# Moving the rare stages of a software-pipelined kernel behind layer 0, and five smaller reorderings beside it

## The chip, the cores and the metric

The kernel runs on one core of a Trainium2 chip. Its engines work side by side, each through its own queue in order, and meet at semaphores: PE (TensorE, matmuls), ACT (ScalarE), DVE (VectorE), POOL (GpSimd), and SP, which here only issues DMAs. The metric is the device time of one execution in microseconds. Before the change it is 1403.78 us, the median of 3 runs (1403.2 to 1403.82).

## The reference

The input `x` is 64 x 64 x 1024 (batches, channels, length), the style vector `cond_512` 64 x 128. A block is computed in two halves.

```python
# half 1: x1 = x + S4(conv1(x));  half 2: out = x1 + FFN(conv2(x1))
for i, typ in enumerate(('same', 'upsample', 'same', 'downsample')):
    s = style @ mw.T + mb                      # modulation
    weight = SCALE * w * s[:, None, :, None]
    demod = rsqrt(sum(weight * weight, (2, 3)) + EPS)
    x = conv(x, weight * demod) + b            # kernel 3, blur of 4 taps
K = ifft(cauchy-kernel of Lambda, p, q, B, C)  # length 1024
y = irfft(rfft(u) * rfft(K)) + D * u           # S4: a causal convolution
```

The four conv layers are linear, with a style per batch. The FFN is a base matrix of 1024 x 1024 with its bias, plus a router that picks 2 of 8 experts of rank 16.

## The kernel before, in words

**Tiles and passes.** A tile is two batches (128 rows of batch and channel), so there are 32 tiles in a pass. The first pass (turns 0 to 31) does conv1 and S4 and keeps x1 in DRAM (`x1d`), the second (32 to 63) conv2 and the FFN. Float32 products are split: a value is held as a high and a low part (`a_h`, `a_l`), and each product is three matmuls, written by `product` (L1625 to L1627).

**The convolution of a tile.** Layer 0 is one product on the input (`xs_h`, `xs_l`) into the bank `ps_x`. Its output, scaled, gives `a_h`, `a_l` and, for sums of neighbouring columns, `a_f`. Layers 1 to 3 are composed on the weights into one filter per batch: `step1` and `step2` on PE with `composed1` (ACT `c_h`, DVE `c_l`) between them, eight `blurs` taps on DVE, a DMA that lays `vv` out as `vm_f`, and `composed2` (ACT `vm_h`, DVE `vm_l`). The filter is applied by `pair` (two batches) and `third`, which needs sums of filters, made by POOL (`pair_sums`, `vm_f`) and split (`vs_h` by ACT, `vs_l` by POOL). POOL's `combined` joins the three results in `vbuf`, ACT's `row_ends` sets the two outer columns, PE's `turn` transposes the tile into `ps_x` (L1742), and ACT and DVE take it from there as `u_h` and `u_l`.

**S4.** K is multiplied as a Toeplitz matrix: `s4` writes a tail, then `ps_p`, then the two halves of `ps_q`. DVE adds each to the residual `xr` as it comes (`residual`: semaphores `x1_tail`, `x1_both`, `x1_ready`).

**Turns.** Every engine runs a `body(i)`, in which work of tiles i-1 to i+2 is interleaved. The order within a body is written by hand, and it is the only thing that orders the work: an engine that waits holds all that is queued behind it. On PE a turn is pair, step2, pair, third, layer 0 of tile i+1, s4 of tile i-1, step1 of tile i+2, transposes of tile i. The transposes and layer 0 share `ps_x`, so they wait for `a_lo` and `as_sum` of tile i+1, and for `v3_fix` (row ends of tile i).

**Rare work.** Some stages run only in a few turns. `edges(i, s)` names the edge group whose stage s falls in turn i: three groups (begun in turns 1, 25 and 36) compute the outermost columns of 32 batches in four small matmuls (`edge_pe0` to `edge_pe3`), each followed by a DVE stage (`edge_ve0` to `edge_ve3`) a little later in the same turn. Group 1 has its PE stages in turns 4 to 7, group 2 in 28 to 31, group 3 in 39 to 42. `style(i, s)` does the same for the styles of the second pass: styles in turn 8, demodulation in 9, `inverse` in 11, `newton` in 12, `scales` and `shifts` in 13, `through` in 14 to 16. POOL's parts are `edge_lay` (stage 2 of an edge group), `squares(1)`, `mats_low(1)` and `tap_sums(1)`. The PE results of all these go to `ps_p`, so `edges_read` holds PE before it writes there again.

**The start.** `first_turns` sets up K (states, resolvents, transfer function, two small transforms, then through DRAM: `kout` to `kpad` to `toep`) among tile 0 and 1. `flipped` multiplies `toep` with a flipped identity, and ACT's and DVE's `toeplitz` split the result.

## Time and profile before

| | |
|---|---|
| median of 3 runs | 1403.78 us |
| the profiled execution | 1403.37 us |
| its span, first to last instruction | 1401.6 us |
| mean granted clock of PE | 0.988 |
| busy: PE, DVE, ACT, POOL | 1350.8, 948.4, 821.7, 794.3 us |
| chain that ended last: PE, DVE, ACT, POOL, issue | 85%, 7%, 4%, 2%, 1% |

The span is what the trace shows; 1.8 us of the execution lie around it. A line of the profile is named by its number in the kernel before, and operands without their buffer numbers. PE's busy time can overlap in pipelined matmuls, so gaps and the distance between equal instructions of two turns say more than the sum. The granted clock is 1.00 for 2.4 GHz and 0.50 for 1.2 GHz.

### The profile page before, as it was taken

What the parts mean: (1) busy time and instruction counts of PE and PEld (TensorE: products, weight loads), DVE (VectorE), ACT (ScalarE), POOL (GpSimd) and SP (SyncE); (2) the same over time, 40 slices, a digit from 0 to 9 for tenths busy, and PEclk for the clock granted to TensorE, in tenths of its full rate; (3) what the DMA queues carried; (4) which work ended last, traced back from release to release, by engine and by line L of the source; (5) the groups of instructions that cost most, each with busy time, mean ns of one, the idle gap of its engine ahead of it and who ended that gap; (6) DMA issues with size and microseconds to landing.
All of it is one profiled execution on the core that took longest, in us unless ns stands there. A gap on an engine that the chain in (4) does not pass through costs nothing.

```text
span 1401.6 us, 23403 instructions
## 1 busy us (share of the span) xinstructions
PE 1350.8 (96%) x8559; PEld 1276.0 (91%) x8559; DVE 948.4 (68%) x2133; ACT 821.7 (59%) x1649; POOL 794.3 (57%) x598
## 2 busy tenths in 40 slices
PE   4689899989999999999999999999999999999998
PEld 3579889989999998899999999999999999999998
DVE  7867887897777779876565766555556555555653
ACT  4467677867888787785454544545445454544530
POOL 6368666656666676565455454554545555454542
PEclk9789999999999999999999999999999999999999
DMA  4234344545445564452443423425243342524322
GB/s 135 74 102 119 93 136 129 147 116 139 134 127 134 152 148 134 119 146 88 118 106 93 128 74 111 110 78 143 74 127 94 106 115 74 145 76 123 99 80 84
DMA packets 85989, 158.64 MB, mean 113 GB/s; under 512 B 26474, under 2 KB 47859, under 8 KB 85747
## 3 DMA queue, kind: packets, MB, share of 16 engines
q1 hardware_dynamic: 84610, 155.18, 39.9%
q10 hardware_dynamic: 1264, 1.96, 0.4%
q8 instruction: 69, 1.13, 0.4%
q14 instruction: 46, 0.37, 0.1%
HBM read 94.18 MB, written 33.56 MB: 91 GB/s over the span
## 4 chain that ended last, share of the span: by engine, by line
PE 85%; DVE 7%; ACT 4%; POOL 2%; issue 1%; DMA 0%; ACTq 0%; DVEq 0%; POOLq 0%
PE psum L1625 27%; PE psum L1627 26%; PE psum L1626 26%; PE psum L1742 4%; DVE vv L1411 1%; DVE a_l L1423 1%; ACT xin L1001 1%; PE psum L271 1%; DVE a_f L1428 1%; ACT u_h L1057 0%; ACT xs_h L1006 0%; DVE de L355 0%; ACT vbuf L1045 0%; POOL xs_l L858 0%; PE psum L1906 0%
## 5 line engine op out<-in xcount | busy, mean ns | idle before, releaser
L833 POOL TENSOR_TENSOR vbuf<-vbuf 128x512 f32<-128x512 f32 x64 | 97.5, 1523 | 303.3 <-ACT vbuf L1052 303.1
L1625 PE MATMUL psum<-wt_h,u_h 128*128 128x386 f32 (+1 forms) x760 | 261.0, 343 | 0.0
L1627 PE MATMUL psum<-wt_h,u_l 128*128 128x386 f32 (+1 forms) x760 | 258.2, 340 | 0.0
L1626 PE MATMUL psum<-wt_l,u_h 128*128 128x386 f32 (+1 forms) x760 | 257.6, 339 | 0.0
L1423 DVE SCALAR_TENSOR_TENSOR a_l<-psum,tabs,a_h 128x512 fp32r<-128x512 f32 x128 | 95.1, 749 | 126.3 <-ACT a_h L1020 125.8
L847 POOL TENSOR_TENSOR vm_f<-vm_f 128x512 f32<-128x512 f32 x64 | 82.8, 1294 | 167.4 <-DVE vm_l L1417 167.4
L1625 PE MATMUL psum<-a_h,vm_h 128*128 128x256 f32 x512 | 154.8, 302 | 4.2 <-ACT vbuf L1045 4.2
L1045 ACT ACTIVATE vbuf<-psum,tabs 128x512 f32<-128x512 f32 x128 | 105.0, 820 | 85.3 <-PE psum L1627 85.2
L1057 ACT ACTIVATE u_h<-psum 128x1024 fp32r<-128x1024 f32 x64 | 65.5, 1024 | 147.5 <-PE psum L1742 147.4
L858 POOL TENSOR_TENSOR xs_l<-xin,xs_h 128x1024 fp32r<-128x1024 f32 x64 | 141.4, 2210 | 12.9 <-ACT xs_h L1006 12.9
L1411 DVE SCALAR_TENSOR_TENSOR vv<-psum,vv 128x192 f32<-128x192 f32 (+2 forms) x384 | 137.2, 357 | 13.2
L1626 PE MATMUL psum<-a_l,vm_h 128*128 128x256 f32 x512 | 146.0, 285 | 0.0
L1627 PE MATMUL psum<-a_h,vm_l 128*128 128x256 f32 x512 | 145.5, 284 | 0.0
L1626 PEld LDWEIGHTS psum<-wt_l,u_h 128*128 128x128 f32 x760 | 143.6, 189 | 1.2
L1625 PEld LDWEIGHTS psum<-wt_h,u_h 128*128 128x128 f32 x760 | 143.6, 189 | 1.3
L1627 PEld LDWEIGHTS psum<-wt_h,u_l 128*128 128x128 f32 x760 | 143.2, 188 | 0.0
L1506 DVE TENSOR_TENSOR xo<-psum,xo 128x250 f32<-128x250 f32 (+2 forms) x90 | 40.6, 506 | 124.6 <-PE psum L1627 124.6
L878 POOL TENSOR_TENSOR xo<-xr,xo 128x1024 f32<-128x1024 f32 x32 | 85.3, 2666 | 63.1 <-DMA xo<-in_b_base_dram 63.1
L1437 DVE TENSOR_TENSOR u_l<-psum,u_h 128x1024 fp32r<-128x1024 f32 x64 | 78.4, 1224 | 54.5 <-ACT xo L1061 38.4
L1625 PEld LDWEIGHTS psum<-a_h,vm_h 128*128 128x128 f32 x512 | 98.1, 192 | 12.5 <-ACT vbuf L1045 11.9
L1625 PE MATMUL psum<-xs_h,m_h 128*128 128x512 f32 x256 | 104.3, 407 | 0.0
L837 POOL TENSOR_TENSOR vbuf<-vbuf 128x512 f32<-128x512 f32 x64 | 98.9, 1546 | 5.0
(306 smaller groups left out, 4056.8 us busy)
## 6 DMA issues: line engine op xcount, KB each, us to landing
vm_f<-vv SPq DMA_DIRECT2D x256, 112.0 KB, 2.6
xin<-in_x_ph_dram SPq DMA_DIRECT2D x32, 512.0 KB, 4.5
xr<-in_x_row_dram SPq DMA_DIRECT2D x32, 512.0 KB, 5.0
x1d<-xr SPq DMA_DIRECT2D x64, 256.0 KB, 3.3
xin<-x1d SPq DMA_DIRECT2D x32, 512.0 KB, 5.1
xr<-x1d SPq DMA_DIRECT2D x64, 256.0 KB, 5.7
xo<-in_b_base_dram SPq DMA_DIRECT2D x32, 512.0 KB, 3.9
out_dram<-xo SPq DMA_DIRECT2D x31, 512.0 KB, 3.0
```

The costliest lines, as they stand in the source:

```text
L833: G.tensor_tensor(v3[:, :, 1:H:2], v3[:, :, 1:H:2], by_odd, ALU.subtract).then_inc(v3_odd, 1)
L837: G.tensor_tensor(v3[:, :, 0:H:2], v3[:, :, 0:H:2], by_odd, ALU.add).then_inc(v3_val, 1)
L847: G.tensor_tensor(vs_f, vm_f[:, :, :, 0, :], vm_f[:, :, :, 1, :], ALU.add).then_inc(vs_sum, 1)
L858: G.tensor_tensor(xs_l[:, :, 1:H + 1], xin[:, :, :], xs_h[:, :, 1:H + 1].bitcast(F32), ALU.subtract).then_inc(in_lo, 1)
L878: G.tensor_tensor(xo[:, :].rearrange("p (n q) -> p n q", q=2), xr[:, :, :].rearrange("p q n -> p n q"), xo[:, :].rearrange("p (n q) -> p n ...
L1045: A(view(vbuf, H * b, (2 * H + b - H * b, 2), (2, Q)), ps_pair.rearrange("p (r m) -> p r m", r=2), ACT.Identity, scale=tab(c, t, b, T_S4), ...
L1411: V.scalar_tensor_tensor(out=to, in0=src[:, k0:k1 + 1:2, :], scalar=BOTH[j], in1=to, op0=ALU.mult, op1=ALU.add).then_inc(blur, 1)
L1423: V.scalar_tensor_tensor(out=by_parity(a_l, b), in0=ps_x[:, b, :].rearrange("p (m r) -> p r m", r=2), scalar=tabs[:, c, T_S1, batch(t, b)] ...
L1437: V.tensor_tensor(u_l[:, :, :, :].rearrange("m k b c -> m b k c"), ps_x[:, :, :].rearrange("m b (k c) -> m b k c", c=C), u_h[:, :, :, :].r ...
L1625: nc.tensor.matmul(to, stat_h, mov_h, start=first_ and n == 0, stop=False, skip_group_check=True)
L1626: nc.tensor.matmul(to, stat_h, mov_l, start=False, stop=False, skip_group_check=True)
L1627: ins = nc.tensor.matmul(to, stat_l, mov_h, start=False, stop=end, skip_group_check=True)
```

## The change

1. **Inserted stages.** On DVE the rare stages are gathered in `inserted(i)`. In the second pass it stands where they stood, ahead of `layer0(i + 1)`; otherwise behind it, ahead of `composed2(i + 1)`. Their PE results go to `ps_late`, the second half of `ps_q`, so PE's test that they are read (`edges_read`) moves from ahead of `s4` to ahead of its last third, and in the second pass to ahead of `ffn(2)`. Their PE stages wait for `x1_ready` in place of `x1_both`.
2. **Residual.** `residual` is cut in two, and `composed1(i + 2)` stands between them.
3. **POOL.** `edge_lay`, `squares(1)`, `mats_low(1)` and `tap_sums(1)` stand behind `combined` and ahead of `pair_sums(i + 1)`; the last two also come in other turns (4 and 8, before 2 and 4).
4. **K's flip** stands ahead of the transposes of tile 0, and ACT's `row_ends(0)` ahead of `column_sums(1)`.
5. **The start.** `pair(0, 1)` comes whole ahead of `transform`, the two thirds go between K's small transforms, layer 0 of tile 1 ahead of `edge_pe3`; DVE's `through(0, 2)` and `variances(0)` come earlier, POOL's `tap_sums(0)` goes ahead of `mats_low(0)`, ACT's `m0_h` ahead of `rate_times_roots`, and SP loads `cm` ahead of `w3`.

```diff
@@ -597,8 +597,10 @@
-    ps_style, ps_demod = (ps_step, ps_p), (ps_p, ps_p)
-    ps_beta = (ps_q[:, 0, :], ps_p)
+
+    ps_late = ps_q[:, 1, :]
+    ps_style, ps_demod = (ps_step, ps_late), (ps_p, ps_late)
+    ps_beta = (ps_q[:, 0, :], ps_late)
...
@@ -646,8 +648,8 @@
                 sp.dma_start(mwT[:, 0, :, :].rearrange("p a b -> p (a b)"), d["mod_w"][:, 0:NL * P]).then_inc(style_in, 16)
+                sp.dma_start(cmf[:, 0, :, :].rearrange("p b c -> p (b c)"), d["cm"][:, 0:NCM * P]).then_inc(cm_in, 16)
                 sp.dma_start(w3T[:, :, :, :].rearrange("p a b c -> p (a b c)"), d["w3"]).then_inc(w3_in, 16)
-                sp.dma_start(cmf[:, 0, :, :].rearrange("p b c -> p (b c)"), d["cm"][:, 0:NCM * P]).then_inc(cm_in, 16)
...
@@ -806,8 +808,8 @@
             squares(0)
+            tap_sums(0)
             mats_low(0)
-            tap_sums(0)
...
@@ -867,8 +869,6 @@
                     pair_sums_low(i)
                 if first(i - 1):
                     sum_low(i - 1)
-                for e in edges(i, 2):
-                    edge_lay(nc, pool, sh, e)
                 if here(i):
                     combined(i)
                 if second(i - 1):
...
@@ -877,6 +877,15 @@
                                     xo[:, :].rearrange("p (n q) -> p n q", q=2), ALU.add).then_inc(xo_ready, 1)
+
+                for e in edges(i, 2):
+                    edge_lay(nc, pool, sh, e)
+                if turn_is(i, 1):
+                    squares(1)
+                if turn_is(i, 4):
+                    mats_low(1)
+                if turn_is(i, 8):
+                    tap_sums(1)
                 if turn_is(i, -1):
                     folded(1, fold1())
                     folded(2, fold3())
...
@@ -890,12 +899,6 @@
                     if here(i + 2):
                         inputs(i + 2)
-                if turn_is(i, 1):
-                    squares(1)
-                if turn_is(i, 2):
-                    mats_low(1)
-                if turn_is(i, 4):
-                    tap_sums(1)
...
@@ -954,9 +957,9 @@
             mats_high(0)
             roots_of(0)
-            rate_times_roots()
             act.wait_ge(m0_in, 16)
             A(m0_h[:, :, :, :], m0f[:, :, :, :], ACT.Copy).then_inc(mats_hi, 1)
+            rate_times_roots()
             act.wait_ge(fold_in, 32)
...
@@ -1086,11 +1089,11 @@
                 third_evacuated(0)
                 layer0(1)
                 composed2(1)
+                row_ends(0)
                 column_sums(1)
                 pads(1)
                 inputs(2)
                 inputs_high(2)
-                row_ends(0)
                 composed1(2)
...
@@ -1452,6 +1457,8 @@
                 ve.wait_ge(s4_both, at(g))
                 V.tensor_tensor(xr[:, :, :], ps_p.unsqueeze(1).to_broadcast([P, 2, H]), xr[:, :, :], ALU.add)\
                     .then_inc(x1_both, 1)
+
+            def residual_last(g):
                 ve.wait_ge(x1_both, at(g))
                 ve.wait_ge(s4_done, at(g))
                 V.tensor_tensor(xr[:, :, :], ps_q[:, :, :], xr[:, :, :], ALU.add).then_inc(x1_ready, 1)
...
@@ -1516,6 +1523,7 @@
                 step_rate()
                 variances(0)
+                step_scaled()
                 inverse(0)
                 newton(0)
...
@@ -1533,12 +1541,12 @@
                 edge_ve0(nc, ve, sh, 0, ps_p)
                 through(0, 1)
                 resolvents()
+                through(0, 2)
                 state_halves()
                 composed1(1)
                 resolvents_scaled()
                 layer0(0)
                 composed2(0)
-                through(0, 2)
                 transfer()
                 edge_ve1(nc, ve, sh, 0, ps_p)
...
@@ -1552,6 +1560,29 @@
+
+            def inserted(i):
+                for e in edges(i, 1):
+                    if e > 1:
+                        ve.wait_ge(sh.edge_in, 64 * (e - 1))
+                    edge_scale(nc, ve, sh, e, sh.xg[:, :, :] if e > 1 else xgA[:, EB:B, :])
+                for k, stage in enumerate((edge_ve0, edge_ve1, edge_ve2, edge_ve3)):
+                    for e in edges(i, 3 + k):
+                        stage(nc, ve, sh, e, ps_late)
+                if style(i, -3):
+                    styles(1)
+                if style(i, -2):
+                    variances(1)
+                if style(i, 0):
+                    inverse(1)
+                if style(i, 1):
+                    newton(1)
+                if style(i, 2):
+                    scales(1)
+                    shifts(1)
+                for l in range(3):
+                    if style(i, 3 + l):
+                        through(1, l)
...
@@ -1576,37 +1607,23 @@
...
-                    if style(i, 3 + l):
-                        through(1, l)
+                if second(i - 1):
+                    inserted(i)
                 if here(i + 1):
                     layer0(i + 1)
+                if not second(i - 1):
+
+                    inserted(i)
                 if second(i - 1):
                     router(place(i - 1)[1])
                 if here(i + 1):
                     composed2(i + 1)
                 if first(i - 1):
-                    residual(i - 1)
+                    residual_first(i - 1)
                 if here(i + 2):
                     composed1(i + 2)
+                if first(i - 1):
+                    residual_last(i - 1)
...
@@ -1758,6 +1766,8 @@
                 if g == 0:
                     pe.wait_ge(toep_lo, 3)
                 for to, done, tb, stat in ((ps_p, s4_both, 0, None), (ps_q[:, 0, :], None, 1, 0), (ps_q[:, 1, :], s4_done, 2, 1)):
+                    if stat == 1:
+                        edges_read(i)
                     for j in range(3):
                         st = (s_h[:, j, :], s_l[:, j, :]) if stat is None else rows(2 * j + stat)
...
@@ -1799,8 +1809,6 @@
                     pe.wait_ge(ssq_ready, 2)
                 if style(i, -2):
                     pe.wait_ge(var_ready, 2)
-                if turn_is(i, 1):
-                    pe.wait_ge(sh.edge_step, sh.edge_read[0, 3])
...
@@ -1820,26 +1828,24 @@
                 resolved()
                 pair(0, 0)
                 step2(1)
+                pair(0, 1)
                 transform()
-                pair_begins(0, 1)
+                third(0, 0)
                 twisted()
-                pair_ends(0, 1)
+                third(0, 1)
                 second_transform()
                 edge_pe2(nc, pe, sh, 0, ps_p)
-                third(0, 0)
-                third(0, 1)
+                layer0(1)
                 pe.wait_ge(folds, 2)
                 edge_pe3(nc, pe, sh, 0, ps_p)
-                layer0(1)
                 pe.wait_ge(blur, at(1, NBLUR, NBLUR - 1))
                 step1(2)
+                flipped()
                 pe.wait_ge(a_lo, at(1, 2, 1))
                 pe.wait_ge(as_sum, at(1))
                 turn(0)
 
             def body(i):
-                if turn_is(i, 1):
-                    flipped()
...
@@ -1854,12 +1860,12 @@
                         if i - 2 < TILES:
-                            pe.wait_ge(x1_both, i - 1)
+                            pe.wait_ge(x1_ready, i - 1)
                         else:
                             pe.wait_ge(out_ready, i - 1 - TILES)
-                        stage(nc, pe, sh, e, ps_p)
+                        stage(nc, pe, sh, e, ps_late)
                 if any(style(i, k) for k in (-3, -2, 3, 4, 5)):
-                    pe.wait_ge(x1_both, i - 1)
+                    pe.wait_ge(x1_ready, i - 1)
...
@@ -1876,8 +1882,9 @@
                 if first(i - 1):
                     if i > 1:
                         pe.wait_ge(x1_ready, i - 1)
-                    edges_read(i)
-                    s4(i - 1)
+                    else:
+                        pe.wait_ge(sh.edge_step, sh.edge_read[0, 3])
+                    s4(i - 1, i)
...
@@ -1889,7 +1896,6 @@
                         pe.wait_ge(out_ready, t)
-                    edges_read(i)
                     (ffn_by_parts(i - 1) if turn_is(i - 1, LAST) else ffn(0)).then_inc(pe_gate, 1)
...
@@ -1920,6 +1926,7 @@
                     else:
+                        edges_read(i)
                         ffn(2)
                         pe.wait_ge(hwT_lo, t + 1)
```

DVE in turn 12, Newton's step. L1186 to L1189 and, in the changed kernel, L1189 to L1192 are `newton(1)`; `a_l`, `a_f` are layer 0 of tile 13, `vm_l` its filter. Before:

```order
L1574 TENSOR_TENSOR wt_l<-wst,wt_h 128x320 [waits w_hi]
L1186 TENSOR_TENSOR dema<-dem 128x256
L1187 TENSOR_TENSOR dema<-dema,demt 128x256 [waits chain]
L1188 TENSOR_SCALAR dema<-dema 128x256 [waits chain]
L1189 SCALAR_TENSOR_TENSOR dem<-dem,dema 128x256 [waits chain]
L1423 SCALAR_TENSOR_TENSOR a_l<-psum,tabs,a_h 128x2x256 [waits a_hi,chain]
L1423 SCALAR_TENSOR_TENSOR a_l<-psum,tabs,a_h 128x2x256 [waits a_hi]
L1428 SCALAR_TENSOR_TENSOR a_f<-psum,tabs,a_f 128x256 [waits a_odd]
L1428 SCALAR_TENSOR_TENSOR a_f<-psum,tabs,a_f 128x256
L1417 TENSOR_TENSOR vm_l<-vm_f,vm_h 128x512 [waits vm_hi] x2
L1449 TENSOR_TENSOR xr<-psum,xr 128x2x128 [waits s4_tail,xr_in]
L1453 TENSOR_TENSOR xr<-psum,xr 128x1024 [waits s4_both,x1_tail]
```

and now:

```order
L1605 TENSOR_TENSOR wt_l<-wst,wt_h 128x320 [waits w_hi]
L1428 SCALAR_TENSOR_TENSOR a_l<-psum,tabs,a_h 128x2x256 [waits a_hi] x2
L1433 SCALAR_TENSOR_TENSOR a_f<-psum,tabs,a_f 128x256 [waits a_odd]
L1433 SCALAR_TENSOR_TENSOR a_f<-psum,tabs,a_f 128x256
L1189 TENSOR_TENSOR dema<-dem 128x256
L1190 TENSOR_TENSOR dema<-dema,demt 128x256 [waits chain]
L1191 TENSOR_SCALAR dema<-dema 128x256 [waits chain]
L1192 SCALAR_TENSOR_TENSOR dem<-dem,dema 128x256 [waits chain]
L1422 TENSOR_TENSOR vm_l<-vm_f,vm_h 128x512 [waits vm_hi,chain]
L1422 TENSOR_TENSOR vm_l<-vm_f,vm_h 128x512 [waits vm_hi]
L1454 TENSOR_TENSOR xr<-psum,xr 128x2x128 [waits s4_tail,xr_in]
L1458 TENSOR_TENSOR xr<-psum,xr 128x1024 [waits s4_both,x1_tail]
```

Newton's four instructions have passed from ahead of `a_l` to between `a_f` and `vm_l`.

POOL in turn 1. `vbuf` is `combined`, `wsq` and `wsqT` are `squares(1)`, `vm_f` is `pair_sums(2)`. Before:

```order
L835 TENSOR_TENSOR vbuf<-vbuf 128x2x255 [waits v3_odd]
L837 TENSOR_TENSOR vbuf<-vbuf 128x512 [waits v3_odd]
L847 TENSOR_TENSOR vm_f<-vm_f 128x2x256 [waits vm_lo]
L862 TENSOR_TENSOR as_l<-a_f,as_h 128x2x256 [waits as_hi]
L858 TENSOR_TENSOR xs_l<-xin,xs_h 128x2x512 [waits in_hi]
L781 TENSOR_TENSOR wsq<-wT 64x768 [waits wT1_in]
L783 TENSOR_TENSOR wsq<-wsq 64x4x64 [waits wsq_step]
L786 TENSOR_TENSOR wsqT<-wsq 64x4x64 [waits wsq_step]
L786 TENSOR_TENSOR wsqT<-wsq 64x4x64
L853 TENSOR_TENSOR vs_l<-vm_f,vs_h 128x512 [waits third_done,vs_hi]
```

and now:

```order
L837 TENSOR_TENSOR vbuf<-vbuf 128x2x255 [waits v3_odd]
L839 TENSOR_TENSOR vbuf<-vbuf 128x512 [waits v3_odd]
L783 TENSOR_TENSOR wsq<-wT 64x768 [waits wT1_in]
L785 TENSOR_TENSOR wsq<-wsq 64x4x64 [waits wsq_step]
L788 TENSOR_TENSOR wsqT<-wsq 64x4x64 [waits wsq_step]
L788 TENSOR_TENSOR wsqT<-wsq 64x4x64
L849 TENSOR_TENSOR vm_f<-vm_f 128x2x256 [waits vm_lo]
L864 TENSOR_TENSOR as_l<-a_f,as_h 128x2x256 [waits as_hi]
L860 TENSOR_TENSOR xs_l<-xin,xs_h 128x2x512 [waits in_hi]
L855 TENSOR_TENSOR vs_l<-vm_f,vs_h 128x512 [waits third_done,vs_hi]
```

The squares have passed from behind `xs_l` to ahead of `pair_sums(2)`.

PE at the end of `first_turns`. `dt,flip` is K's flip, `ident,vbuf` the transposes of tile 0, `a_h,vm_h` the first pair of tile 1. Before:

```order
L1626 MATMUL psum<-x_l,cm_h 128x192
L1627 MATMUL psum<-x_h,cm_l 128x192
L1742 MATMUL psum<-ident,vbuf 128x128 [waits v3_fix,as_sum,a_lo]
L1742 MATMUL psum<-ident,vbuf 128x128 x7
L1675 MATMUL psum<-dt,flip 128x512 [waits toep_in]
L1675 MATMUL psum<-dt,flip 128x512
L1625 MATMUL psum<-a_h,vm_h 128x256 [waits vm_lo,vm_hi,a_pad]
```

and now:

```order
L1643 MATMUL psum<-x_l,cm_h 128x192
L1644 MATMUL psum<-x_h,cm_l 128x192
L1692 MATMUL psum<-dt,flip 128x512 [waits toep_in]
L1692 MATMUL psum<-dt,flip 128x512
L1750 MATMUL psum<-ident,vbuf 128x128 [waits v3_fix,as_sum,a_lo]
L1750 MATMUL psum<-ident,vbuf 128x128 x7
L1642 MATMUL psum<-a_h,vm_h 128x256 [waits vm_lo,vm_hi,a_pad]
```

The flip, which waits for K's DMA, now stands ahead of the transposes.

## Rows read from the trace of the kernel before

**Rows 1.** Waits of PE: engine, line, waited for, total us, times, longest us.

```profile
PE psum L1625 <- POOL vs_l L853: 4.5, 2, 2.4
PE psum L1625 <- DVE c_l L1384: 4.3, 5, 1.1
```

**Rows 2.** Timeline of PE: start us, us, instruction, count, idle before and releaser; L1742.

```profile
72.07 1.94 PE L1742 MATMUL psum<-ident,vbuf 128*128 128x128 f32 x8 [5.28 <-ACT vbuf L1038]
...
93.27 1.04 PE L1742 MATMUL psum<-ident,vbuf 128*128 128x128 f32 x8
...
129.46 1.04 PE L1742 MATMUL psum<-ident,vbuf 128*128 128x128 f32 x8
...
204.02 1.04 PE L1742 MATMUL psum<-ident,vbuf 128*128 128x128 f32 x8
...
270.07 1.04 PE L1742 MATMUL psum<-ident,vbuf 128*128 128x128 f32 x8
...
323.35 1.04 PE L1742 MATMUL psum<-ident,vbuf 128*128 128x128 f32 x8
...
388.38 1.04 PE L1742 MATMUL psum<-ident,vbuf 128*128 128x128 f32 x8
...
532.04 1.04 PE L1742 MATMUL psum<-ident,vbuf 128*128 128x128 f32 x8
...
603.17 1.04 PE L1742 MATMUL psum<-ident,vbuf 128*128 128x128 f32 x8
```

**Rows 3.** Chain that ended last, second pass, L1742: start us, us, what.

```profile
766.62 0.87 PE psum L1742 x8
...
869.64 0.87 PE psum L1742 x8
...
894.23 0.87 PE psum L1742 x8
```

**Rows 4.** Timelines of DVE, POOL and PE in a steady turn of the first pass.

```profile
397.97 0.75 DVE L1423 SCALAR_TENSOR_TENSOR a_l<-psum,tabs,a_h 128x512 fp32r<-128x512 f32 x1 [1.64 <-ACT a_h L1020]
...
400.02 0.87 DVE L1428 SCALAR_TENSOR_TENSOR a_f<-psum,tabs,a_f 128x256 f32<-128x256 f32 x2
...
400.81 1.28 DVE L1417 TENSOR_TENSOR vm_l<-vm_f,vm_h 128x512 fp32r<-128x512 f32 x2
...
391.46 1.29 POOL L853 TENSOR_TENSOR vs_l<-vm_f,vs_h 128x512 fp32r<-128x512 f32 x1 [0.64 <-ACT vs_h L995]
...
402.17 1.30 POOL L847 TENSOR_TENSOR vm_f<-vm_f 128x512 f32<-128x512 f32 x1 [1.43 <-DVE vm_l L1417]
...
393.67 0.28 PE L1625 MATMUL psum<-as_h,vs_h 128*128 128x256 f32 x1
```

**Rows 5.** DVE: L1187 twice in its timeline, then busy time in four windows.

```profile
18.67 0.43 DVE L1187 TENSOR_TENSOR dema<-dema,demt 128x256 f32<-128x256 f32 x1
...
278.39 1.63 DVE L1187 TENSOR_TENSOR dema<-dema,demt 128x256 f32<-128x256 f32 x1
...
19.90:21.35 1.45, 1.30 (x8) 1.00 0.00 0
23.08:24.20 1.12, 1.02 (x7) 1.00 0.03 7
159.25:164.30 5.05, 4.83 (x8) 1.00 0.04 13
295.70:301.55 5.85, 5.64 (x15) 1.00 0.53 148
```

**Rows 6.** The start: SP's and PE's timelines, then PE, granted clock in a window.

```profile
63.97 0.34 SPq L668 DMA_DIRECT2D dt<-kpad  x1
...
73.81 3.52 PE L1675 MATMUL psum<-dt,flip 128*128 128x512 f32 x4
...
81.04 0.39 PE L1625 MATMUL psum<-a_h,vm_h 128*128 128x256 f32 x1 [0.96 <-ACT vbuf L1045]
...
70.00:72.00 2.00, 0.00 (x0) 0.57 0.00 0
```

More of the change, by code:

```diff
@@ L1284, in step_rate, with step_scaled @@
                 link(V.tensor_scalar(stpi[:, :], stpi[:, :], 23, None, ALU.logical_shift_left))
+            def step_scaled():
                 V.tensor_tensor(rate, stpi[:, :].bitcast(F32), pp, ALU.mult).then_inc(rate_ready, 1)
@@ L1444, in even_and_odd, with residual_first @@
                                 s_odd.rearrange("m j b c -> m b j c"), ALU.add).then_inc(sum_ready, 1)
-            def residual(g):
+            def residual_first(g):
                 ve.wait_ge(xr_in, 16 * (g + 1))
@@ L1578, in body @@
                                            op0=ALU.mult, op1=ALU.subtract).then_inc(bt_lo, 1)
-                for e in edges(i, 1):
-                    if e > 1:
-                        ve.wait_ge(sh.edge_in, 64 * (e - 1))
-                    edge_scale(nc, ve, sh, e, sh.xg[:, :, :] if e > 1 else xgA[:, EB:B, :])
-                for k, stage in enumerate((edge_ve0, edge_ve1, edge_ve2, edge_ve3)):
-                    for e in edges(i, 3 + k):
-                        stage(nc, ve, sh, e, ps_p)
-                if style(i, -3):
-                    styles(1)
-                if style(i, -2):
-                    variances(1)
-                if style(i, 0):
-                    inverse(1)
-                if style(i, 1):
-                    newton(1)
-                if style(i, 2):
-                    scales(1)
-                    shifts(1)
-                for l in range(3):
-                    if style(i, 3 + l):
-                        through(1, l)
+                if second(i - 1):
+                    inserted(i)
                 if here(i + 1):
                     layer0(i + 1)
+                if not second(i - 1):
+                    inserted(i)
                 if second(i - 1):
@@ L1706, in step2, with pair @@
                 ins.then_inc(step2_done, 1)
-            def pair_begins(g, b):
+            def pair(g, b):
                 if b == 0:
@@ L1715, in pair_begins @@
                 pe.wait_ge(vm_lo, at(g, 2, b))
-                columns(g, b, 0)
-            def columns(g, b, r):
-                o = (EVEN, 1)[r]
-                return product(ps_pair[:, Q * r:Q * r + Q],
-                               [(vm_h[:, b, P * (2 * k + r):P * (2 * k + r) + P], vm_l[:, b, P * (2 * k + r):P * (2 * k + r) + P],
-                                a_h[:, b, o + k:o + k + Q], a_l[:, b, o + k:o + k + Q]) for k in range(2)], True, True)
-            def pair_ends(g, b):
-                columns(g, b, 1).then_inc(pair_done, 1)
-            def pair(g, b):
-                pair_begins(g, b)
-                pair_ends(g, b)
+                for r, o in ((0, EVEN), (1, 1)):
+                    ins = product(ps_pair[:, Q * r:Q * r + Q],
+                                  [(vm_h[:, b, P * (2 * k + r):P * (2 * k + r) + P], vm_l[:, b, P * (2 * k + r):P * (2 * k + r) + P],
+                                    a_h[:, b, o + k:o + k + Q], a_l[:, b, o + k:o + k + Q]) for k in range(2)], True, True)
+                ins.then_inc(pair_done, 1)
             def third(g, b):
@@ L1746, in rows, with s4 @@
                 return (u_h[:, k, :, :].rearrange("p b c -> p (b c)"), u_l[:, k, :, :].rearrange("p b c -> p (b c)"))
-            def s4(g):
+            def s4(g, i):
                 pe.wait_ge(pair_out, at(g + 1, 2, 1))
```

## Prediction

> **What bounds the kernel now.** The waits of the tensor engine come first: PE is busy for 1350.8 of 1401.6 us (the page), and its single waits are short [rows 1]. Then the starts of its eight transposes, once a turn, say where those waits lie [rows 2]. From 388.38 to 532.04 us nine turns take 143.66 us: 15.96 us a turn, gapless, so in an undisturbed turn only matmuls count, and nothing here removes a matmul. The loss lies in five places, each worked out against 15.96 a turn.
> - The start: transposes of tile 0 at 72.07, after 5.28 us idle.
> - Turns 2 and 3 (93.27 to 129.46): 36.19, so 4.3 too long, 3.8 of it in turn 2.
> - Turns 4 to 7, the first edge group (129.46 to 204.02): 74.56, less 4 x 15.96, 10.7 too long. The same four edge stages cost PE 4.7 as pure matmul work in the second pass: from 766.62 to 869.64 is 103.02 against 4 x 24.59 [rows 3]. So 6.0 is waiting.
> - Turns 12 to 14, Newton's step, scales and shifts (270.07 to 323.35): 53.28 less 47.88 is 5.4, of which about 0.6 is the constant's own matmuls: 4.8.
> - Turns 28 to 31, the second edge group (532.04 to 603.17): 71.13 less 63.84 less 4.7 is 2.6.
> Together with the start some 22 us are to be had, no more.
>
> **The inserted stages.** In a steady turn whose transposes start at 388.38, the order on the vector engine is a_l, column sums a_f (end 400.89, 12.5 after the transposes), vm_l (end 402.09), residual; then POOL's pair_sums, as_l, xs_l and vs_l follow from vm_l. POOL starts vs_l of this chain after an idle of 0.64, and has it 0.92 before PE begins the third that reads it (391.46 + 1.29 = 392.75 against 393.67) [rows 4]. So a stage of length X put between a_f and vm_l holds PE by X - 1.56. Before, X stood ahead of a_l: there idle times of the vector engine (1.64 ahead of the first a_l [rows 4], 0.64 ahead of the second) swallow 2.3 of it, but what is left delays a_f, on which the transposes, ACT's column sums, the next inputs and c_h hang; PE then waited for c_l [rows 1].
> By that alone the new place is worse for equal X, since it has no idle time to hide in. What decides is X itself. The same instruction (L1187, 128x256) took 0.43 us when POOL was quiet and 1.63 beside POOL's combination of a tile [rows 5]. The scales and shifts took 1.45 and 1.12 at the start, and 5.85 as one piece in turn 13; the second stage of an edge took 5.05 in turn 5 [rows 5]. The new place lies where POOL has finished the combination and waits for vm_l, so I take the quiet durations: 2.6 for scales and shifts; for the edge stages, Newton and the like the same ratio (2.6/5.85 = 0.44) gives 2.2 for the 5.05, and about 2.1 each for the first edge stage and Newton. The others are under 1.8. The bounds are both ends of the ratio, 0.44 and 1.
> Waiting after: 0.6 + 0.6 + 0.1 per edge group, call it 1.5 with small change; 1.0 for scales, 0.5 for Newton, 0.2 for the reciprocal: 1.7. Gains: first edge group 6.0 - 1.5 = 4.5 (its worst wait, 2.4 for vs_l [rows 1], came from tap_sums, see below); turns 12 to 14: 4.8 - 1.7 = 3.1; second edge group 2.6 - 1.5 = 1.1. Sum 8.7.
> The Trainium skill (SBUF, State Buffer; section Who interferes with whom) gives a reason for the two durations: VectorE and GpSimd share a port pair as an exclusive lock, and a vector instruction with two SBUF inputs blocks against a GpSimd instruction that reads SBUF, for its whole length. L1187 agrees. The same rule speaks against the change at POOL's moved pieces, below.
>
> **POOL's moved pieces.** squares(1) (3.8 us behind xs_l, the cause of turn 2's wait of 2.1 for vs_l), mats_low(1), tap_sums(1) and the edge layouts now stand between the combination and pair_sums, where POOL idles 1.4 in a steady turn [rows 4]. What is longer pushes pair_sums and so vs_l, with 1.56 allowed. squares(1): 3.8 - 1.4 = 2.4 late, stall 0.8 without interference; beside vm_l (two instructions, 1.28 together [rows 4]) up to 1.3 more. I take a stall of 1.5: 0.6 gained. Turn 2's other 1.7 is clock: the idle before it was followed by a stretch at half clock as in [rows 6]; with a wait still there I count half of it back. Gain 1.4 (0.3 to 3.0). mats_low and tap_sums now fall into turns whose inserted stage delays vm_l anyway, at 0 to 0.8. The edge layouts (about 3 us) had idle time ahead of the combination and lose it: 3.0 - 1.4 - 1.56 is 0, with vm_l's 1.28 in it 1.3, at two turns. I take 1.2 for all of this, range 0 to 3.5. By the skill's rule taken at its word the upper ends hold, and this part alone would come to about +2.
>
> **The residual.** composed1's c_l now runs ahead of the last sum. Steady: c_l at 405.1 to 405.65, last sum to 406.9, and the next u_l starts at 406.9 (390.97 one turn on). It fits without a gap; 0, and if it did not, u_l has several us until layer 0. SP's x1 store starts 1.9 later, its reader is a turn off. The tests of the edge banks move from the head of the S4 product into its third part, 3.9 us later, which covers the later reads; the second pass keeps its order.
>
> **The start.** Three small things: variances no longer wait for step_scaled, POOL has tap_sums done before Newton's multiply, so the scales come 2 to 3 us earlier, but ACT, busy without a gap from 14.1 to 21.7, allows only 0.9 of it. through(0,2) leaves a crowded place and costs 0.9 in a quiet one instead of 2.5. The transfer function so starts about 2.1 earlier, and K's way with it, since blurs(1), which SP's vm copies and then K's DMAs follow, ends on the same chain. pair(0,1), 2.9 us on PE, goes into PE's wait of 3.3 us for atv. K's second DMA was issued at 63.97 [rows 6], with 3.4 to landing in the list of DMAs: 67.4, now about 65.3. PE has nothing from about 62 on, and K's flip, now ahead of tile 0's transposes, holds these till K is there. Flip 3.5 [rows 6] at half clock (the level of 1.2 GHz), 1.8 at full; transposes 1.9 [rows 2] or 1.0. ACT's row_ends(0), moved ahead of inputs(2), is no longer what they wait for. They end at 68.0 to 70.6, ACT's u_h then follows, and with toeplitz() behind it the evacuation that PE's next pair needs ends 5.0 later: 73.2 to 75.7 instead of 81.0 [rows 6]. Gain 5.3 to 7.8; I take 6.0, near the half-clock end, because the clock fell to half 4 us into the idle before [rows 6].
>
> **The sum.** 8.7 + 1.4 - 1.2 + 6.0 = 14.9; turn 3's half us comes back, 0.3: 15.2. The profiled execution took 1403.37 (span 1401.6 and 1.8 around it), 0.4 under the median 1403.78. So 1388.4.
>
> **Rivals.**
> A, the late chain: the inserted stages keep their long durations. Then behind a_f they cost 4.7 - 1.56, 5.05 - 1.56, 2.0 and so on: 8 per edge group against 6.0 and 2.6, and 3.3 + 4.3 against 4.8 in turns 12 to 14. That is 10 worse than before, and each of about six waits over 2 us may pull the clock to half for 2.7 us, 1.4 lost each, 8 in all. Against it 7.4 from start and turn 2: 1403.4 + 18 - 7.4 = 1414. It decides from an average X of about 3.5, where it would be even. For it: every one of these stages was long in the trace. Against it: POOL idle there.
> B, K holds the transposes: the DVE chain does not shorten, K lands at 67.4 as before, flip and transposes run at half clock to 72.8, gain at the start 3; POOL's pieces at their upper end, 3.5: total gain 3 + 0.3 + 8.7 - 3.5 = 8.5, so 1394.9.
> C, everything goes well: clock at full through the start (7.8), turn 2 wholly cured (3.8), edge layouts free (0): 8.7 + 7.8 + 3.8 + 1.5 = 21.8 and 1381.6.
> D, no change: the freed time is taken by another wait, c_l and x1_tail both, which have 1.0 and 2.7 of room. Stage lengths around 3.5, within 0.2%.
>
> **Chances.** Forecast 0.58, B 0.17, C 0.14, A 0.06, D 0.05. A difference under 0.2% (2.8 us) can't be told from none. Faster 0.91, same 0.04, slower 0.05. The range reaches from C to B: 1381.5 to 1396.
>
> **What would show it.** Right: transposes of tile 0 at 66 to 69 with the flip in front; turn 2 within 18.3; turns 4 to 7 together at 70; Newton's L1187 line at 0.4 us; PE's waits for vs_l short but more of them, those for c_l nearly gone. Wrong: vector copies over 0.6 us behind a_f, waits for vm_l or for x1_tail, or a steady turn above 16.0.

## The result, and the profile after

The changed kernel takes 1426.67 us (median of 4 runs, 1426.44 to 1426.93), the kernel before 1403.49 (4 runs, 1403.15 to 1403.82): a ratio of 1.0165 [1.0148, 1.0183]. The forecast was 1388.4, with a range to 1396.0. The profiled execution has a span of 1424.8 us, 23.2 more than before, at a mean granted clock of 0.994.

The chain of waits of the changed kernel, shares of the span by engine and then by line. Before, PE had 85% of it.

```profile
PE 56%; DMA 14%; ACT 10%; DVE 10%; SPq 4%; issue 4%; POOL 2%; ACTq 0%; DVEq 0%; POOLq 0%
PE psum L1642 18%; PE psum L1644 17%; PE psum L1643 17%; DMA vm_f<-vv 10%; DMA x1d<-xr 4%; SPq L723 3%; ACT xin L1004 2%; DVE vv L1416 2%; PE psum L1750 2%; ACT xs_h L1009 2%; DVE xr L1464 2%; ACT as_h L994 1%; ACT c_h L983 1%; DVE u_l L1442 1%; SPq L680 1%
```

DMAs, which had 0% before, now hold 14%: the copies of the blurred filter (`vm_f<-vv`) and the store of x1 (`x1d<-xr`). PE's waits say the same from its side, beside [rows 1] (line, waited for, total us, times, longest us):

```profile
PE psum L1642 <- DVE c_l L1389: 17.5, 21, 1.1
PE psum L1642 <- ACT vbuf L1048: 12.1, 28, 2.2
PE psum L1642 <- POOL vs_l L855: 2.6, 3, 1.6
```

Then PE's transposes in turns where nothing rare happens, which before stood 15.96 apart [rows 2]:

```profile
424.94 1.06 PE L1750 MATMUL psum<-ident,vbuf 128*128 128x128 f32 x8
443.22 0.95 PE L1750 MATMUL psum<-ident,vbuf 128*128 128x128 f32 x7 [0.38 <-ACT vbuf L1041]
461.40 0.85 PE L1750 MATMUL psum<-ident,vbuf 128*128 128x128 f32 x6 [0.27 <-ACT vbuf L1041]
```

18.28 and 18.18 us (x7 and x6: records that are missing from the trace). From turn 17 to turn 27 each turn is 1.1 to 2.3 longer than before, 1.8 on average. One such turn on SP's queue, on DVE and on ACT (rows left out are marked):

```profile
447.91 1.27 SPq L680 DMA_DIRECT2D x1d<-xr  x2
449.23 0.67 SPq L700 DMA_DIRECT2D xin<-in_x_ph_dram  x1
452.32 0.33 SPq L705 DMA_DIRECT2D xr<-in_x_row_dram  x1
452.75 2.44 SPq L723 DMA_DIRECT2D vm_f<-vv  x4
...
443.44 1.22 DVE L1458 TENSOR_TENSOR xr<-psum,xr 128x1024 f32<-128x1024 f32 x1
446.20 0.55 DVE L1389 SCALAR_TENSOR_TENSOR c_l<-psum,tabp,c_h 128x320 fp32r<-128x320 f32 x1 [1.54 <-ACT c_h L983]
446.67 1.22 DVE L1464 TENSOR_TENSOR xr<-psum,xr 128x1024 f32<-128x1024 f32 x1
...
450.11 2.32 DVE L1416 SCALAR_TENSOR_TENSOR vv<-psum,vv 128x256 f32<-128x256 f32 x6
...
464.37 0.55 DVE L1389 SCALAR_TENSOR_TENSOR c_l<-psum,tabp,c_h 128x320 fp32r<-128x320 f32 x1 [1.62 <-ACT c_h L983]
...
459.04 1.40 ACT L990 ACTIVATE vm_h<-vm_f 128x512 fp32r<-128x512 f32 x2 [3.08 <-DMA vm_f<-vv]
```

It is a closed loop. From `c_l` (446.20) DVE goes on to the last sum, `u_l` and the blurs; these end at 452.43, and SP issues the copies at 452.75, 6.55 behind `c_l`. ACT's `vm_h` waits for them and starts at 459.04, 6.29 later. From there ACT works without a wait through its inputs to `c_h`, and the next `c_l` starts at 464.37, 5.33 behind `vm_h`. 6.55 + 6.29 + 5.33 = 18.17, a turn (18.18). The x1 store hangs on the same `c_l`: the last sum stands behind it, the store is issued at 447.91, SP issues the load of `xr` when the store has landed (452.32), and the copies right behind that load. Before, the same two paths were these:

```profile
386.50 1.22 DVE L1453 TENSOR_TENSOR xr<-psum,xr 128x1024 f32<-128x1024 f32 x1
...
389.14 0.55 DVE L1384 SCALAR_TENSOR_TENSOR c_l<-psum,tabp,c_h 128x320 fp32r<-128x320 f32 x1 [0.16 <-ACT c_h L980]
...
393.28 2.31 DVE L1411 SCALAR_TENSOR_TENSOR vv<-psum,vv 128x256 f32<-128x256 f32 x6
...
389.01 1.27 SPq L678 DMA_DIRECT2D x1d<-xr  x2
390.84 0.33 SPq L698 DMA_DIRECT2D xin<-in_x_ph_dram  x1
393.08 0.33 SPq L703 DMA_DIRECT2D xr<-in_x_row_dram  x1
395.63 2.52 SPq L721 DMA_DIRECT2D vm_f<-vv  x4
```

From the sum before the last to the store it was 389.01 - 386.50 = 2.51, and it is 447.91 - 443.44 = 4.47 now: the split sends the store 1.96 later. What SP waited for between 400 and 550 us, before and then after:

```profile
SPq L703 <- DMA x1d<-xr: 17.6, 9, 2.1
SPq L721 <- DVE vv L1411: 17.4, 9, 2.1
```

```profile
SPq L705 <- DMA x1d<-xr: 17.4, 8, 2.4
```

Before, SP had the load of `xr` out and then stood 1.9 us a turn ready to issue the copies, waiting for DVE's blurs. After, that wait is gone: the load goes out just when the blurs end, and the copies right behind it. Medians of the eleven steady turns 17 to 27, in us; the last column is experiment 3 below:

| | before | changed | 3 |
|---|---|---|---|
| `c_l` to the issue of the copies | 6.48 | 6.29 | 6.49 |
| end of the blurs to that issue | 0.03 | 0.06 | 0.03 |
| issue of `xr`'s load to that issue | 2.44 | 0.45 | -2.46 (behind it) |
| issue of the copies to `vm_h` | 3.65 | 6.29 | 3.64 |
| `vm_h` to the next `c_l` | 5.87 | 5.14 | 5.88 |
| turn | 15.96 | 17.76 | 16.00 |

So the copies are not issued late: at most 0.50 behind the end of the blurs in the changed kernel, 0.14 on average. They land late, `vm_h` starts 2.6 us later behind their issue than before, when the 512 KB of `xr` go out 0.45 ahead of them. With the old 3.65 the loop would be 6.29 + 3.65 + 5.14 = 15.1 (an estimate from the table) and would hide under PE's 15.96. The profile's chain of waits goes through the x1 store in 12 turns between 230 and 630 us and through DVE's blurs in 10; the slow copies are in all of them.

### The profile page after: what moved, and what is told of

Same layout as the page of the kernel before. It is cut to its first block, busy times and chain, and to the rows that moved or that the text cites. A ratio compares the mean times of both kernels' runs of the same rounds, so it can differ in the third digit from the quotient of the medians.

```text
span 1424.8 us, 23407 instructions
## 1 busy us (share of the span) xinstructions
PE 1353.3 (95%) x8559; PEld 1274.1 (89%) x8559; DVE 916.6 (64%) x2133; ACT 817.1 (57%) x1649; POOL 795.6 (56%) x598
## 3 DMA queue, kind: packets, MB, share of 16 engines
q10 hardware_dynamic: 1264, 1.96, 0.4%
q8 instruction: 69, 1.13, 0.3%
## 4 chain that ended last, share of the span: by engine, by line
PE 56%; DMA 14%; ACT 10%; DVE 10%; SPq 4%; issue 4%; POOL 2%; ACTq 0%; DVEq 0%; POOLq 0%
PE psum L1642 18%; PE psum L1644 17%; PE psum L1643 17%; DMA vm_f<-vv 10%; DMA x1d<-xr 4%; SPq L723 3%; ACT xin L1004 2%; DVE vv L1416 2%; PE psum L1750 2%; ACT xs_h L1009 2%; DVE xr L1464 2%; ACT as_h L994 1%; ACT c_h L983 1%; DVE u_l L1442 1%; SPq L680 1%
## 5 line engine op out<-in xcount | busy, mean ns | idle before, releaser
L835 POOL TENSOR_TENSOR vbuf<-vbuf 128x512 f32<-128x512 f32 x64 | 97.5, 1524 | 297.8 <-ACT vbuf L1055 297.8
L990 ACT ACTIVATE vm_h<-vm_f 128x512 fp32r<-128x512 f32 x128 | 76.8, 630 | 80.4 <-DMA vm_f<-vv 79.6
L1422 DVE TENSOR_TENSOR vm_l<-vm_f,vm_h 128x512 fp32r<-128x512 f32 x128 | 85.0, 703 | 28.8 <-ACT vm_h L990 28.1
```

The source lines that it names most:

```text
L835: G.tensor_tensor(v3[:, :, 1:H:2], v3[:, :, 1:H:2], by_odd, ALU.subtract).then_inc(v3_odd, 1)
L990: A(vm_h[:, b, :], vm_ff[:, b, :], ACT.Copy).then_inc(vm_hi, 1)
L1422: V.tensor_tensor(vm_l[:, b, :], vm_ff[:, b, :], vm_h[:, b, :].bitcast(F32), ALU.subtract).then_inc(vm_lo, 1)
```

## The experiments

The names: S, the split closes the loop through SP's queue; P, the inserted stages behind layer 0 are the loss; D, `c_l` ahead of the last sum hurts on DVE itself. All ratios are to the kernel before, run on the same chip. This D is not rival D of the prediction.

**1. The change, the last sum whole again.**

```diff
-                if here(i + 2):
-                    composed1(i + 2)
                 if first(i - 1):
                     residual_last(i - 1)
+                if here(i + 2):
+                    composed1(i + 2)
```

> The changed kernel, but the residual's last sum stands ahead of composition's low part again; all else as changed. Theory S (the split closes a loop through SP: last sum, x1 store, its completion, xr load, vm copies, vm_h, vm_l, c_h, c_l, last sum, about 18 us long in the changed kernel's trace): the first pass goes back to 15.96 us a turn, 26 turns x about 1.1 to 1.8 come back, 1395 to 1402. Rival P (the inserted stages and POOL's pieces behind layer 0 are what lengthens the turns): it stays at 1420 or above.

1394.41 us (1393.52 to 1395.13), ratio 0.9943 [0.9926, 0.996]. Steady turns take 15.96 to 16.03. That is 0.6 under the range expected. Two lines in another order cost 32.3 us (the kernel before took 1403.27 beside this run and 1403.49 beside the change); P is refuted, and the rest of the change is worth about 9.

**2. The split alone, in the kernel before.** `residual` cut in two with `composed1` between, nothing else.

```diff
                 if first(i - 1):
-                    residual(i - 1)
+                    residual_first(i - 1)
                 if here(i + 2):
                     composed1(i + 2)
+                if first(i - 1):
+                    residual_last(i - 1)
```

> The kernel before, with nothing changed but the split of the residual: composition's low part ahead of the last sum. Theory S: undisturbed turns of the first pass rise from 15.96 to 17.5 to 18.2 us, total 1425 to 1440. Rival P: within 3 us of the kernel before.

1434.11 us (1433.41 to 1434.63), ratio 1.0227 [1.0209, 1.0245]. PE's transposes of two steady turns:

```profile
414.76 1.06 PE L1746 MATMUL psum<-ident,vbuf 128*128 128x128 f32 x8
432.52 1.04 PE L1746 MATMUL psum<-ident,vbuf 128*128 128x128 f32 x8
450.87 1.06 PE L1746 MATMUL psum<-ident,vbuf 128*128 128x128 f32 x8 [0.46 <-ACT vbuf L1038]
```

17.76 and 18.35: the loop is there without any other part of the change, with the same numbers (load to copies 0.45, copies to `vm_h` 6.30).

**3. The change with its split; on SP the load of `xr`, with its wait for the store, goes behind the copies.** The arithmetic engines' orders are those of the change.

```diff
-                if first(i - 1):
-                    _, t = place(i - 1)
-                    if t:
-                        sp.wait_ge(x1_out, 32 * t)
-                    sp.dma_start(xr[:, :, :], ...)
...
                                          vv[HALF[b], :, :]...).then_inc(vm_in[b], 16)
+                if first(i - 1):
+                    _, t = place(i - 1)
+                    if t:
+                        sp.wait_ge(x1_out, 32 * t)
+                    sp.dma_start(xr[:, :, :], ...)
```

> The changed kernel with its split, but on SP the xr load (with its wait for the end of the x1 store) is issued behind the vm copies in place of ahead of them. Theory S: the loop is open, DVE's copies' wait falls away, turns of 16.0 to 16.4 us, 1397 to 1410, though the residual then waits for xr. Rival D (the split costs on DVE itself, by the later u_l and blurs, not through SP): turns stay at 17.5 and more, 1420 or above.

1392.80 us (1392.13 to 1393.45), ratio 0.9931 [0.9914, 0.9948]. SP's queue in a steady turn, and PE:

```profile
379.70 1.28 SPq L680 DMA_DIRECT2D x1d<-xr  x2
381.02 0.68 SPq L700 DMA_DIRECT2D xin<-in_x_ph_dram  x1
384.49 2.92 SPq L718 DMA_DIRECT2D vm_f<-vv  x4
387.45 0.58 SPq L724 DMA_DIRECT2D xr<-in_x_row_dram  x1
...
425.23 1.04 PE L1750 MATMUL psum<-ident,vbuf 128*128 128x128 f32 x8
441.22 1.04 PE L1750 MATMUL psum<-ident,vbuf 128*128 128x128 f32 x8
```

The time is 4 us under the range expected. The copies wait for the blurs again and the turn is 15.99. D is refuted, since DVE's order is the same here. S holds in that the cost comes through SP's queue: the split is harmless once the load that waits for its store stands behind the copies. The median time from issue to landing of one copy went with it, from 4.4 in the changed kernel (2.6 before) to 2.3 here:

```profile
vm_f<-vv SPq DMA_DIRECT2D x36, 112.0 KB, 4.4
```

```profile
vm_f<-vv SPq DMA_DIRECT2D x40, 112.0 KB, 2.3
```

The table above separates two parts of the cure. The time of issue gave little, 0.14 us a turn on average. The landing gave 2.6. That it is the 512 KB right ahead that slow the copies rests on their nearness in time in these kernels; no run changes the size of that load, so what is shared stays open.

**4. As 1, with two edits of the start undone:** `mats_low(0)` ahead of `tap_sums(0)` on POOL, SP's `w3` ahead of `cm`.

> As the run with the last sum ahead, and besides POOL's mats_low(0) ahead of tap_sums(0) and SP's w3 ahead of cm, as in the kernel before. If DVE's ssq (2.56 us in the changed kernel, 0.42 before) was held by POOL's row of tap sums, ssq falls back to 0.4 to 0.6 and everything up to tile 0 comes about 2 us earlier: 1 to 2.5 us under the run with the last sum ahead. If the 2 us come from elsewhere, no difference.

1393.93 us (1392.37 to 1394.36), ratio 0.9938 [0.9925, 0.9952]: no difference from 1 that could be told. The transposes of tile 0 come 1.1 earlier (69.42 for 70.52), but those of tile 1 only 0.4.

**5 to 8: parts alone.** 5 is the kernel before with part 1 of the change, 6 with parts 4 and 5, 7 is experiment 1 with part 3 undone, 8 is experiment 1 with SP's copies first.

> The kernel before with part 1 of the change alone: the inserted stages behind layer 0, their PE results in ps_late, the tests of the edge banks and the waits for x1_ready with it. The prediction gave this part 8.7 us (first edge group 4.5, turns 12 to 14 3.1, second edge group 1.1), so 1394.6. Read from the trace of the change with the whole sum (first edge group 71.03 us for 74.56, turns 12 to 14 50.65 for 53.28, second group 71.13 for 71.13, turn 9 0.5 longer) it is worth 3.5 + 2.6 + 0 - 0.5 = 5.6, so 1397.7, and somewhat less here, since tap_sums(1) still stands behind xs_l in turn 4 and holds the same vs_l that an inserted stage holds: 1397.7 to 1400. The rival theory that inserted stages behind layer 0 cost (late chain) says 1404 or more.

> The kernel before with the start alone: K's flip ahead of tile 0's transposes, row_ends(0) early, and all of part 5. The prediction gave it 6.0 us: 1397.3. Read from the trace of the change with the whole sum, the first pair of tile 1 starts at 76.55 for 81.04 (4.5 earlier), but the transposes of tile 1 start at 90.26 for 93.27 (3.0 earlier), so 1.5 of it is given back in turn 0 to waits for DVE and SP that the flip had covered: 3.0, and 1400.3. The rival of the prediction in which K alone holds the transposes says 3.0 as well, with the flip waiting for K's DMA; it differs in that the first pair would start 3 earlier, not 4.5.

> The change with the whole sum, and POOL's moves undone: edge_lay ahead of combined, squares(1), mats_low(1), tap_sums(1) behind xs_l in turns 1, 2 and 4. If POOL's moves bring what the prediction gave turn 2 and cost what it gave the layouts (1.4 and 1.2), the time stays within 1 us of the 1394.4 of the change with the whole sum, with turn 2 near 20.2 instead of 18.65 us and a turn with an edge layout shorter. If the moves matter more (tap_sums(1) in turn 4 behind xs_l plus an inserted stage), it is 1396 to 1398. If the gap between the gains predicted (14.9) and found (9) lies in POOL's pieces, it is 1391 or less.

> The change with the whole sum, and SP's load of xr with its wait for the x1 store behind the vm copies. If the loop through SP's queue was the only thing that the split cost, then with copies first it no longer matters where the sum stands: 1392.8 to 1394.4, the 1392.8 of the split with copies first plus up to 1.6 for PE's few waits for c_l, which the split had cured. If the early xr load itself (its own wait for the store) cost something in the change with the whole sum too, this is clearly below 1394.4, at 1391 to 1392.5. If the xr load comes too late behind the copies, steady turns exceed 16.0 and it is above 1395.

| | us | ratio | turn of 146.55 before |
|---|---|---|---|
| 5, inserted stages alone | 1402.83 (1398.59 to 1404.47) | 1.0002 [0.9989, 1.0015] | 23.62 |
| 6, start alone | 1400.72 (1397.53 to 1402.31) | 0.9988 [0.9977, 0.9999] | 20.21 |
| 7, both, POOL as before | 1401.68 (1397.02 to 1403.66) | 0.9996 [0.9982, 1.001] | 23.56 |
| 8, all with the whole sum, copies first | 1394.38 (1392.16 to 1397.02) | 0.9948 [0.9931, 0.9964] | 17.53 |
| before | 1402.84 (1399.03 to 1404.6) | 1 | 21.78 |

The expectations of 6 and 8 came. That of 5 was missed (1397.7 to 1400), and all three of 7 (the highest was 1398): the inserted stages alone bring nothing. POOL's moves are worth 7 us in the presence of the others, and one turn holds 6.1 of it (23.56 for 17.50 in experiment 1).

**9 to 11: POOL's moves apart.** 9 is experiment 3 with `edge_lay` back ahead of `combined`; 10 is the kernel before with `tap_sums(1)` alone moved, from behind `xs_l` in turn 4 to behind `combined` in turn 8; 11 is 5 with the same move.

```diff
+                if turn_is(i, 8):
+                    tap_sums(1)
...
-                if turn_is(i, 4):
-                    tap_sums(1)
```

> The change with SP's copies first, and the edge layouts back ahead of POOL's combination; the other moves of POOL stay. The turn with a layout took 17.64 us with the layout behind the combination and 17.08 with it ahead (two turns, the groups that begin in turns 1 and 25), so this should save 0.56 at each: 1392.8 less 1.1 is 1391.7. The prediction's price was up to 1.3 at each of two turns: then 1390.2. If the combination delayed by the layout costs elsewhere (row ends, transposes), 1393 to 1394.

> The kernel before, with tap_sums(1) alone moved: from behind xs_l in turn 4 to behind the combination in turn 8. In the traces so far turn 4 took 21.78 us before, 23.62 and 23.56 with the inserted stages behind layer 0 and tap_sums in its old place, 17.50 with both moved. If the two costs are simply added at vs_l, taps alone bring 21.78 less 17.5 less what the stage ahead of a_l still costs (about 1 us), 3.3, less 0.45 in turn 8: 1400.5. If the stage ahead of a_l was all that the turn lost, nothing: 1403.3. If tap_sums was the whole loss, 4.3 less 0.45: 1399.5.

> The kernel before, with the inserted stages behind layer 0 and tap_sums(1) behind the combination in turn 8. The inserted stages alone gave 1402.8 (no gain); the pair should give turn 4 its 6.1 us (23.6 to 17.5) less 0.45 in turn 8: 5.6, so 1397.2. If the 6.1 came from another of POOL's moves (the layouts, mats_low), it stays at 1402.

Before took 1402.31 (1398.93 to 1405.35) here. 9: 1391.82 (1390.1 to 1396.51), ratio 0.9914 [0.99, 0.9928]; the two turns with a layout shrink by just about the 0.56 expected, from 17.64 to 17.04 and from 17.64 to 17.07. 10: 1398.26 (1396.73 to 1402.75), 0.9976 [0.9963, 0.9989], nearest to the case in which tap_sums was that turn's whole loss (1399.5). 11: 1397.6 (1396.53 to 1398.93), 0.9965 [0.9947, 0.9982], as expected. The turn of the tap sums, in POOL's timeline before and in 10, with PE's wait before:

```profile
153.73 1.26 POOL L853 TENSOR_TENSOR vs_l<-vm_f,vs_h 128x512 fp32r<-128x512 f32 x1
...
155.13 0.35 PE L1625 MATMUL psum<-as_h,vs_h 128*128 128x256 f32 x1 [2.37 <-POOL vs_l L853]
```

```profile
149.40 1.28 POOL L853 TENSOR_TENSOR vs_l<-vm_f,vs_h 128x512 fp32r<-128x512 f32 x1
```

`vs_l` started 7.18 behind the transposes (146.55), behind four groups of sums that nobody needed for turns and that had begun at 150.27, 3.46 earlier; in 10 it starts 3.82 behind them (145.58), and the turn is 17.60 for 21.78. This 4.2 is more than the wait of 2.37: behind that wait PE's granted clock was 0.50 from 156 to 159 us, and in 10 it stays at 1.00. Turns 6 and 9 give 0.8 and 0.7 of it back, so over the first pass the move brings 3.1 (543.72 for 546.86 us from the transposes of tile 0 to those 32 turns on). The inserted stages add 2.7 to it: over the same stretch 10 takes 543.72 us (71.53 to 615.25) and 11 takes 540.98 (71.25 to 612.23).

**12. The version to which this points:** 9 with the two edits of the start undone as in 4.

> The version that the experiments point to: the residual split, SP's copies first, the edge layouts ahead of the combination, and, of the start, POOL's tap_sums(0) back behind mats_low(0) and SP's cm back behind w3. With the sum whole these two edits of the start brought 0.5 (1393.9 for 1394.4), and they take away the runs in which the first squares of DVE met POOL's reads (2.56 us for 0.42 in the trace of the change). So 1391.3, with less spread than the 1390.1 to 1396.5 of the version with the layouts back. If the late start of that version's profiled run comes from something else (a DMA of the start), the spread stays and the median is 1391.8 or above.

1391.71 us (1390.95 to 1392.72), ratio 0.9927 [0.9912, 0.9942]. It beats both kernels, before by 0.73% and the change by 35 us. Its runs lie within 1.8 us, those of 9 within 6.4; but those of 3, whose start is that of 9, lie within 1.3, so the smaller spread is not shown to come from the start. The time lies between the two expected values. Against 3 and 9 it can't be told apart by its time.

## Why the prediction was wrong

**The step that failed** is "The residual": "It fits without a gap; 0, and if it did not, u_l has several us until layer 0. SP's x1 store starts 1.9 later, its reader is a turn off." The 1.9 was right (1.96), and so was DVE's part: `c_l` to the copies takes 6.3 for 6.5. What hangs on the store was left out: the load of `xr` waits for that very store, 2.2 us in each turn on SP, so it now goes out 0.45 ahead of the copies of the next filter and not 2.44. The copies then take 6.3 to `vm_h` in place of 3.7, and a path that had room under PE's 15.96 becomes a loop of 17.8. I followed the data to its reader in the second pass and the semaphore to nobody. Priced at 0, the term was worth +32.3 (1426.67 less 1394.41), more than all other terms together. In the traces 28.8 of this lie in the first pass and 1.8 in the turn behind it; the other 1.7 lie ahead of tile 0's transposes (72.21 for 70.52), where both kernels have the same code (`ssq` took 2.56 in the one and 0.52 in the other, see the last section). None of the rivals had it; A had the right side at a chance of 0.06, by a mechanism that the runs refute.

**The second step that failed** is the division between "The inserted stages" and "POOL's moved pieces". The first had 8.7 and alone brought nothing (experiment 5, ratio 1.0002), since tap_sums held the same `vs_l`; with that one out of the way they add 2.7 (11 against 10). The second had +1.4 - 1.2 and brought 7 (1 against 7). The start had 6.0 and alone brought 2.1 (6). Part of the forecast gain came, but from POOL's moves and not from the stages behind layer 0 by themselves.

**The other terms**, from PE's transposes in experiment 1 against [rows 2]; the parts sum to the 9.3 by which the transposes at 618.93 come earlier (609.60):

| stretch, before | predicted gain | found |
|---|---|---|
| start, to 93.27 | 6.0 | 3.01 (90.26) |
| turn 2, its squares | 1.4 | 1.13 (18.65 for 19.78) |
| turn 3 | 0.3 | 0.14 |
| first edge group | 4.5 | 3.53 (71.03 for 74.56) |
| turns 12 to 14 | 3.1 | 2.63 (50.65 for 53.28) |
| second edge group | 1.1 | 0.04 (71.09 for 71.13) |
| POOL's pieces; found: all that is in no other row | -1.2 | -1.15 (turn of tap_sums 17.66 for 17.20, the rest in steps under 0.2) |

That the last row agrees is luck: the -1.2 was meant mostly for the edge layouts, which fall into the two edge groups. Of 15.2, 9.3 came. *Inserted stages.* Their quiet lengths were forecast well. Newton's second instruction, the scales with shifts (2.6 forecast) and the second DVE stage of an edge (2.2 forecast), in experiment 1:

```profile
276.26 0.42 DVE L1190 TENSOR_TENSOR dema<-dema,demt 128x256 f32<-128x256 f32 x1
...
292.21:294.72 2.51, 2.31 (x15) 1.00 0.01 4
156.79:159.24 2.45, 2.31 (x8) 1.00 0.00 1
```

The 0.42 stands for 1.63 in [rows 5]. That answers rival A. But behind the whole sum they delay `c_l` as well, not only `vs_l`: in the first edge group PE waits 1.8 for `c_l` and 0.4 for `vs_l`, and only with the split and copies first (experiment 3) is it `vs_l` alone, 1.5 in all, the figure forecast. So the split does do something: it takes PE's waits for `c_l` away. It needs SP's order changed with it. The layouts cost 0.6 at each of two turns; I had them at up to 1.3. Turn 2 has a wait of 1.56 for `vs_l` behind the squares, the 1.5 forecast, and one of 0.81 for `c_l` that was not forecast:

```profile
93.53 0.41 PE L1642 MATMUL psum<-c_h,cm_h 128*128 128x320 f32 x1 [0.81 <-DVE c_l L1389]
98.17 0.36 PE L1642 MATMUL psum<-as_h,vs_h 128*128 128x256 f32 x1 [1.56 <-POOL vs_l L855]
```

*The start.* K's DMA is issued at 63.61 for the 63.97 of [rows 6], not 2.1 earlier. Scales were ready 1.6 earlier, but DVE's next step waited for ACT, which did not come earlier:

```profile
19.50 0.19 DVE L1206 COPY tabs<-dem 128x64 f32<-128x64 f32 x1
...
22.60 0.42 DVE L1382 SCALAR_TENSOR_TENSOR x_l<-w3T,tabp,x_h 128x192 fp32r<-128x192 f32 x1 [2.91 <-ACT x_h L977]
```

Before, this step started at 22.29. I had allowed ACT 0.9 of gain; it gave 0.3 of loss, since `m_h` ahead of its work waits 0.59 for a DMA. So K and not the row ends held the transposes, as rival B had it:

```profile
67.25 3.43 PE L1692 MATMUL psum<-dt,flip 128*128 128x512 f32 x4 [3.89 <-DMA dt<-kpad]
70.52 1.04 PE L1750 MATMUL psum<-ident,vbuf 128*128 128x128 f32 x8
...
76.55 0.39 PE L1642 MATMUL psum<-a_h,vm_h 128*128 128x256 f32 x1 [2.23 <-ACT vbuf L1048]
```

The first pair starts 5.0 behind the end of the transposes, as forecast, so 4.5 earlier than before. Then 1.5 goes again: PE's granted clock (third column behind the busy time) in that stretch and behind it was

```profile
77.10:80.40 3.30, 3.30 (x18) 0.50 0.02 5
81.00:90.00 9.00, 9.00 (x54) 1.00 0.23 51
```

The matmuls of 256 columns that stood 0.12 apart before stand 0.21 apart for 3.3 us behind the wait of 2.23. 4.5 less 1.5 is the 3.0 of the table.

*Signs named beforehand.* Newton at 0.4: right. "a steady turn above 16.0" as the sign of being wrong: it was the one that came. Turn 2 within 18.3: 18.65 in experiment 1; 17.76 in the change and also in experiment 4, which has the whole sum, so the split is not what makes that difference. Turns 4 to 7 at 70: 71.0 in experiment 1, 72.1 in the change. PE's waits for `c_l` "nearly gone": 17.5 us in the change for 4.3 before. "Transposes of tile 0 at 66 to 69": 70.52.

*Sums.* The five places of loss add up to 23.0 and not 22; 15.2 under 1403.37 is 1388.2; and 1.5 of rival C's 21.8 has no source in the text. None of these changes the outcome.

## What to carry to other kernels

When a result is produced later, list who waits for the *semaphore* of each consumer's DMA, and what is queued behind that wait on the same queue. A delayed store delays the load behind it, and a large load that comes to stand right ahead of small copies can cost more by their landing (2.6 us here) than by their issue (0.14). Walk such a path once around: if it ends where it began, the turn can't be shorter than the loop, however much room each engine seems to have. Work that nobody needs soon should never stand ahead of a small step that another engine waits for: the turn that gained most (4.2 us) had 3.46 us of it moved away.
